# Expert loop of an attention and mixture-of-experts layer: more row and result slots, one bank for row transposes, result summed in 256 columns

## The reference

```python
x = x + attention(layernorm(x), wq, wk, wv, wo)      # 16 heads of 128, rotary, causal
h = layernorm(x)                                      # 2048 rows of 256
scores = softmax(h @ gate_w.T)                        # 8 experts
topk_w, topk_idx = top_k(scores, 2); topk_w /= topk_w.sum(-1)
y_all[e] = (silu(h @ w1[e]) * (h @ w3[e])) @ w2[e]    # 176 inner columns
y = sum over the two chosen experts of topk_w * y_all
x = x + y + (silu(h @ sw1) * (h @ sw3)) @ sw2         # shared part, 352 inner columns
```

## Time and profile before

| | us |
|---|---|
| median of 3 runs | 754.27 |
| all runs | 753.98, 754.27, 758.5 |
| span of the profiled execution | 754.1 |
| TensorE busy in it | 721.8 (96%) |
| VectorE busy | 641.8 (85%) |
| ScalarE busy | 535.6 (71%) |
| GpSimd busy | 513.2 (68%) |

### The profile page before, as it was taken

How to read it: one execution, slowest core, us unless ns; L and a number is a source line. 1 busy time by engine, 2 the same in 40 slices (tenths; PEclk the granted TensorE clock), 3 DMA queues, 4 the chain that set the end, 5 groups by cost and what they waited for, 6 DMA issues and landing times.

```text
span 754.1 us, 16244 instructions
## 1 busy us (share of the span) xinstructions
PE 721.8 (96%) x5403; PEld 682.9 (91%) x5403; DVE 641.8 (85%) x1826; ACT 535.6 (71%) x1683; POOL 513.2 (68%) x536
## 2 busy tenths in 40 slices
PE   5899999999999999999999999999999798899998
PEld 4787999999999999999999999999999787689898
DVE  6898889988998989898989988999889757688667
ACT  5788777777777777778777777777777735466474
POOL 5778567777778777877787777777766515544363
PEclk9999999999999999999999999999999999999999
DMA  6545203331322133213312330213444533334371
GB/s 205 147 159 147 100 22 112 117 112 36 118 105 101 37 128 118 80 59 133 131 45 75 134 104 22 83 51 114 183 178 163 199 102 106 112 127 125 124 277 64
DMA packets 49483, 85.90 MB, mean 114 GB/s; under 512 B 8440, under 2 KB 40152, under 8 KB 47800
## 3 DMA queue, kind: packets, MB, share of 16 engines
q1 hardware_dynamic: 45352, 73.44, 29.1%
q0 software_dynamic: 4048, 11.42, 4.2%
HBM read 60.12 MB, written 44.59 MB: 139 GB/s over the span
## 4 chain that ended last, share of the span: by engine, by line
PE 80%; DVE 9%; ACT 4%; POOL 3%; issue 2%; DMA 1%; SPq 0%; another core or an unknown queue 0%; POOLq 0%; DVEq 0%; ACTq 0%
PE bank L642 62%; PE bank L682 5%; PE bank L675 3%; PE bank L691 3%; DVE work L1018 2%; POOL work L473 1%; PE bank L896 1%; PE bank L867 1%; PE bank L898 1%; DVE work L1011 1%; PE bank L886 1%; ACT work L1433 1%; PE bank L790 1%; DVE w_lo L985 1%; PE bank L835 1%
## 5 line engine op out<-in xcount | busy, mean ns | idle before, releaser
L1639 POOL TENSOR_TENSOR qkt_lo<-work,qkt_hi 128x512 fp32r<-128x512 f32 x128 | 166.2, 1298 | 84.1 <-ACT qkt_hi L1426 84.0
L473 POOL TENSOR_TENSOR work<-work 128x512 f32<-128x512 f32 x127 | 165.4, 1303 | 47.1 <-DVE work L1018 44.1
L1018 DVE TENSOR_TENSOR work<-bank,sinn 64x512 f32<-64x512 f32 x256 | 176.2, 688 | 3.4
L642 PE MATMUL bank<-xnt_hi,w_lo 128*128 128x256 f32 x512 | 146.4, 286 | 2.3 <-DVE xnt_lo L1049 2.3
L1426 ACT CAST qkt_hi<-work 128x512 fp32r<-128x512 f32 x128 | 79.6, 622 | 96.3 <-POOL work L473 94.6
L642 PE MATMUL bank<-xnt_lo,w_hi 128*128 128x256 f32 x512 | 145.9, 285 | 0.0
L642 PE MATMUL bank<-xnt_hi,w_hi 128*128 128x256 f32 x512 | 145.8, 285 | 0.0
L1433 ACT ACTIVATE work<-work,bias 128x128 f32<-128x128 f32 (+1 forms) x256 | 112.6, 441 | 0.0
L1011 DVE TENSOR_TENSOR work<-bank,cosn 128x512 f32<-128x512 f32 x128 | 87.9, 687 | 18.6 <-PE bank L642 18.2
L642 PEld LDWEIGHTS bank<-xnt_hi,w_lo 128*128 128x128 f32 x512 | 98.8, 193 | 3.1 <-DVE xnt_lo L1049 3.1
L642 PEld LDWEIGHTS bank<-xnt_lo,w_hi 128*128 128x128 f32 x512 | 99.2, 194 | 0.0
(11 more groups left out here) (182 smaller groups left out, 2140.0 us busy)
## 6 DMA issues: line engine op xcount, KB each, us to landing
rows_by_expert<-in_zero_t SPq DMA_DIRECT2D x17, 1028.0 KB
weights_split<-stage SPq DMA_DIRECT2D x40, 176.0 KB
w_lo<-weights_split SPq DMA_DIRECT2D x4, 1408.0 KB
stage<-rows_by_expert SPq DMA_DIRECT2D x39, 128.5 KB
w_lo<-results_by_token SPq DMA_DIRECT2D x16, 256.0 KB, 4.8
w_hi<-weights_split SPq DMA_DIRECT2D x2, 1536.0 KB
stage<-in_L_ffn_w SPq DMA_DIRECT2D x32, 88.0 KB
weights_split<-stage SPq DMA_DIRECT2D x20, 128.0 KB
```

The lines of the kernel that those rows point to most:

```text
L473: eng.tensor_tensor(roped[:, a], rope_cos[:, a], rope_sin[:, a], ALU.add).then_inc(rope_add, 1)
L642: mm = pe.matmul(out, lhs[a], rhs[b], start=start and n == 0, stop=stop and n == 2, skip_group_check=more)
L1018: op = nc.vector.tensor_tensor(rope_sin[lo:lo + 64, a], p_qk[a][hi:hi + 64, :, :], sn, ALU.mult)
L1639: nc.gpsimd.tensor_tensor(qkt[a][1][:, :, :], roped[:, a], qkt[a][0][:, :, :], ALU.subtract).then_inc(qkt_lo, 1)
```

## The change

- Twelve places for rows (`ESLOTS`). The first four lie in `stage` as before; the other eight lie in the low half of the attention's output weights, so the fifth fetch waits for the last `output` (`y_ps`). Only four tiles are fetched ahead of the second plan's constants and of the rows of the next four shared tiles; the others follow these.
- Eight places for results (`YSLOTS`); the added four lie in `stage`.
- `turn_x` uses one bank (6), and waits for `low_x` of the tile before. All of the last router moves to bank 7, its steps move to iterations 1, 2 and 7, and the waits at L857 to L864 go; `turn_rows(8, 1)` and `ranks` have their own.
- `down_e` is five matmuls of 256 columns into one sum: hi by w2 high, hi by w2 low, lo by w2 high, the stack of 112 rows by w2 high, and the 48 high rows by w2 low. VectorE's addition goes; ScalarE's copy takes columns 0 to 255 and is the whole `result`.
- `plan_tiles` is cut into seven parts, for the second plan in iterations 9 to 15. The first plan runs the same instructions in the same three places.
- The rows of t = 3 are split in iteration 35, those of t = 4 in iteration 37.
- GpSimd's order: `results_out` 0; `later_first`, `sooner_first`; 1, 2; `choose`; 3, 4; `weigh`; 5; `address`; the four `send`; then 6 to 38.

```diff
-TURN, GATE, RANK = 2, 3, 9
+TURN, GATE, RANK = 1, 2, 7
-ESLOTS = 8
+ESLOTS, NEAR = 12, 4
+YSLOTS = 8
...
-        p_turn = [cut(3, P), cut(6, P)]
+        p_turn = [cut(3, P), cut(7, P)]
...
-        p_xe = [cut(6, P), cut(7, P)]
+        p_xe = cut(6, P)
...
             def tile_in(j):
+                if j == NEAR:
+                    sp.wait_ge(y_ps, B * N)
                 if j >= ESLOTS:
-                    sp.wait_ge(y_out[j % XSLOTS], 16 * ((j - ESLOTS) // XSLOTS + 1))
+                    sp.wait_ge(y_out[(j - ESLOTS) % YSLOTS], 16 * ((j - ESLOTS) // YSLOTS + 1))
...
-            for j in range(ESLOTS):
+            for j in range(NEAR):
                 tile_in(j)
             sp.wait_ge(max_done[1], B * N)
             sp.dma_start(plan_at[1][:, 0:DCONST], plan_t).then_inc(plan_in, 16)
             for t in range(S1, S1 + XSLOTS):
                 rows_in(t)
-            for j in range(ESLOTS, NF):
+            for j in range(NEAR, NF):
                 tile_in(j)
...
             def turn_x(j):
-                if j == 1:
-                    pe.wait_ge(resid_done, B)
-
-                if j == TURN + 2:
-                    pe.wait_ge(xt2_cp, B)
-                if j == GATE + 2:
-                    pe.wait_ge(logit_done, B)
-                if j == RANK + 2:
-                    pe.wait_ge(place_done, 2 * B)
+                if j >= 1:
+                    pe.wait_ge(xe_lo, j)
                 pe.wait_ge(x_got[j % ESLOTS], 16 * (j // ESLOTS + 1))
...
-                pe.matmul(p_yy[a][:, :], act_e[0][:, a, 0, :], downs_e[:, bass.ds(e, 1), 0, :], start=True, stop=False)
-                pe.matmul(p_yy[a][:, 0:D], act_e[1][:, a, 0, :], downs_e[:, bass.ds(e, 1), 0, 0:D], start=False, stop=False)
-                pe.matmul(p_yy[a][:, :], act_e[0][0:64 + E_TAIL, a, 1, :], downs_e[0:64 + E_TAIL, bass.ds(e, 1), 1, :],
-                          start=False, stop=True).then_inc(ye_ps, 1)
+                y = p_yy[a][:, 0:D]
+                hi, lo = act_e[0][:, a, 0, :], act_e[1][:, a, 0, :]
+                pe.matmul(y, hi, downs_e[:, bass.ds(e, 1), 0, 0:D], start=True, stop=False)
+                pe.matmul(y, hi, downs_e[:, bass.ds(e, 1), 0, D:2 * D], start=False, stop=False)
+                pe.matmul(y, lo, downs_e[:, bass.ds(e, 1), 0, 0:D], start=False, stop=False)
+                both, tail = act_e[0][0:64 + E_TAIL, a, 1, :], act_e[0][0:E_TAIL, a, 1, :]
+                pe.matmul(y, both, downs_e[0:64 + E_TAIL, bass.ds(e, 1), 1, 0:D], start=False, stop=False)
+                pe.matmul(y, tail, downs_e[0:E_TAIL, bass.ds(e, 1), 1, D:2 * D], start=False, stop=True).then_inc(ye_ps, 1)
...
-            def result(j):
-
-                dve.wait_ge(half_done, j + 1)
-                nc.vector.tensor_tensor(y_slot[j % XSLOTS], y_slot[j % XSLOTS], p_yy[j % 2][:, 0:D], ALU.add).then_inc(ye_cp, 1)
...
-                if j == NJ - 1:
-                    rows_low(S1)
+                if j in (NJ - 4, NJ - 2):
+                    rows_low(S1 + (j - NJ + 4) // 2)
...
-                if j in range(RANK + 1, RANK + 5):
-                    plan_tiles(1, j - RANK - 1)
+                if j in range(RANK + 2, RANK + 9):
+                    plan_tiles(1, j - RANK - 2)
...
-            def half(j):
+            def result(j):
 
                 act.wait_ge(ye_ps, j + 1)
-                if j >= XSLOTS:
-                    act.wait_ge(y_out[j % XSLOTS], 16 * (j // XSLOTS))
-                nc.scalar.copy(y_slot[j % XSLOTS], p_yy[j % 2][:, D:2 * D]).then_inc(half_done, 1)
+                if j >= YSLOTS:
+                    act.wait_ge(y_out[j % YSLOTS], 16 * (j // YSLOTS))
+                nc.scalar.copy(y_slot[j % YSLOTS], p_yy[j % 2][:, 0:D]).then_inc(ye_cp, 1)
...
             for n in range(TOP * ST):
                 send((xn2, twin)[n // ST][:, n % ST, :], n // ST, n % ST)
-                results_out(RANK + n)
-            for j in range(RANK + TOP * ST, NJ):
+            for j in range(6, NJ):
                 results_out(j)
```

More of the change, by code:

```diff
@@ L165, in build @@
         stage_all = stage[:, :, :].rearrange("p a b -> p (a b)")
-        assert ESLOTS * RW + DC * P <= NSTAGE * CH
+        results_at = NEAR * RW
+        rows_at = results_at + (YSLOTS - 4) * D
+        assert rows_at + DC * P <= NSTAGE * CH
         xs_slot = [t.rearrange("p (c s) -> p c s", c=DC)
-                   for t in (stage_all[:, ESLOTS * RW:ESLOTS * RW + DC * P], cosn[:, :], sinn[:, :], work[:, 0:DC * P])]
+                   for t in (stage_all[:, rows_at:rows_at + DC * P], cosn[:, :], sinn[:, :], work[:, 0:DC * P])]
         xs_t = [t[:, :].rearrange("p (a c s) -> p a c s", a=2, c=DC) for t in xnt_all]
@@ L173, in build @@
         acts_e = work[:, 2048:2048 + 4 * P].rearrange("p (a m) -> p a m", a=2)
-        x_slot = [stage_all[:, n * RW:(n + 1) * RW] for n in range(ESLOTS)]
-        y_slot = [v_late[n // 2][:, n % 2 * D:(n % 2 + 1) * D] for n in range(XSLOTS)]
+        far = G * GE
+        assert (ESLOTS - NEAR) * RW <= N * D
+        x_slot = [stage_all[:, n * RW:(n + 1) * RW] for n in range(NEAR)]
+        x_slot += [whl[1][:, far + n * RW:far + (n + 1) * RW].bitcast(F32) for n in range(ESLOTS - NEAR)]
+        y_slot = [v_late[n // 2][:, n % 2 * D:(n % 2 + 1) * D] for n in range(4)]
+        y_slot += [stage_all[:, results_at + n * D:results_at + (n + 1) * D] for n in range(YSLOTS - 4)]
         scaled = [stage_all[:, n * TOP * D:(n + 1) * TOP * D] for n in range(XSLOTS)]
+        assert XSLOTS * TOP * D <= rows_at
         twin = work[:, DC * P:DC * P + ST * RW].rearrange("p (t d) -> p t d", t=ST)
@@ L325, in build @@
         ye_cp = sem("ye_cp")
-        y_out = [sem(f"y_out{a}") for a in range(XSLOTS)]
+        y_out = [sem(f"y_out{a}") for a in range(YSLOTS)]
         came = [sem(f"came{a}") for a in range(NT)]
@@ L617, in result_in @@
                 sp.dma_start(back[t], src).then_inc(came[t], 16)
-            for n in range(XSLOTS):
-                sp.wait_ge(y_out[n], 16 * len(range(n, NJ, XSLOTS)))
+            for n in range(YSLOTS):
+                sp.wait_ge(y_out[n], 16 * len(range(n, NJ, YSLOTS)))
             for t in range(NT):
@@ L1105, in sequence @@
                             plan_tiles(0, 0)
+                            plan_tiles(0, 1)
                         if h == 12:
                             rows_low(1)
-                            plan_tiles(0, 1)
-                        if h == 13:
                             plan_tiles(0, 2)
                             plan_tiles(0, 3)
+                        if h == 13:
+                            for part in range(4, 7):
+                                plan_tiles(0, part)
                             mult_s(0)
@@ L1267, in plan_tiles @@
                                                  steps[:, None, :].to_broadcast([P, E, 16]), ALU.is_gt))
+                if part == 1:
                     step(nc.vector.tensor_reduce(tiles, over, AX.X, ALU.add))
@@ L1273, in plan_tiles @@
                         step(nc.vector.tensor_tensor(rest, tiles, taken[:, 0:E], ALU.subtract))
-                if part == 1:
+                if part == 2:
                     step(nc.vector.tensor_tensor(sums, (rest if late else tiles)[:, None, :].to_broadcast([P, E, E]), upto,
@@ L1286, in plan_tiles @@
                                                  ALU.mult))
-                if part == 3:
+                if part == 5:
                     step(nc.vector.tensor_reduce(tile_d, held, AX.X, ALU.add))
@@ L1290, in plan_tiles @@
                         step(nc.vector.tensor_scalar(tile_d, tile_d, taken[:, 0:1], 1.0, ALU.subtract, ALU.mult))
+                if part == 6:
                     nc.vector.tensor_scalar(result[:, 0, :], tile_x, float(E - 1), 1.0, ALU.min, ALU.mult).then_inc(done, 1)
@@ L1525, in high_x @@
                 act.wait_ge(xe_ps, j + 1)
-                nc.scalar.copy(xe_t[0][:, j % 2], p_xe[j % 2][:, 0:DC, :]).then_inc(xe_hi, 1)
+                nc.scalar.copy(xe_t[0][:, j % 2], p_xe[:, 0:DC, :]).then_inc(xe_hi, 1)
             def silu_e(j):
@@ L1591, in _ @@
                     high_x(j + 1)
-                if j == NJ - 1:
-                    rows_high(S1)
+                if j in (NJ - 4, NJ - 2):
+                    rows_high(S1 + (j - NJ + 4) // 2)
                 silu_e(j)
@@ L1599, in _ @@
                 if j >= 2:
-                    half(j - 2)
+                    result(j - 2)
                 if j == GATE:
@@ L1611, in _ @@
             silu_s(S1)
-            half(NJ - 2)
-            half(NJ - 1)
-            rows_high(S1 + 1)
+            result(NJ - 2)
+            result(NJ - 1)
             for t in range(S1 + 1, NT):
@@ L1792, in _ @@
             results_out(0)
-            results_out(1)
             later_first(B)
             sooner_first(B)
+            results_out(1)
             results_out(2)
+            choose(B)
             results_out(3)
             results_out(4)
-            choose(B)
-            for j in range(5, RANK - 1):
```

(3 more changed lines are left out.)

17 lines of the change are left out of this document (7 added, 10 removed).

## The result

The changed kernel took 764.99 us as the median of 4 runs (763.72 to 765.74), beside 756.22 us for the kernel before in the same comparison (4 runs, 753.98 to 758.5); the ratio of the runs is 1.0109, with a 95% interval of 1.0081 to 1.0138. In two later measurements it took 758.61 us (8 runs, beside 752.52 for the kernel before, ratio 1.0065, interval 1.0037 to 1.0092) and 756.83 us (one run, beside 753.89). So the change cost 1.1% in the first comparison and 0.65% in the second, where 745.5 us were forecast and the range ended at 755.

The account below looks back on a forecast made before the run. TensorE was taken as the bound, with 10.3 us of the loop stretch not its work. 754.1 - 10.3 - 1.4 + 0.8 + 0.2 + 1.6 = 745.0, rounded up by 0.5 to 745.5 us; 8-in-10 range 743 to 755 us.

Parts of the forecast that it names:

- `down_e`, 3 to 5 matmuls: Expert loop: five matmuls cost +0.02 us a tile, +0.8 us over 39; the 48-row matmul costs nothing extra.
- the rival: Fifth matmul of `down_e`: a restart at each 48-row matmul, 0.20 us a tile, 753.3 us; with 0.32, 758; chance 0.25.
- The bound: Price of the 48-row matmul from above: 2 x 0.10 us, 0.20 a tile; by the record's length 2 x 0.16, 0.32.
- the sum: Whole kernel: 754.1 - 10.3 - 1.4 + 0.8 + 0.2 + 1.6 = 745.0 us, counted from the profiled execution.
- All of the loop's non-work goes: Expert loop, iterations 2 to 36: the 10.3 us of the 81.2 us stretch that are not TensorE's work go.
- ScalarE's stops: Two "issue" waits, late ScalarE starts: 1.6 us kept in the sum; rival that they remain or move, 749.5 us, chance 0.12.
- Addition of VectorE: Expert loop: 16.4 us of VectorE work go, worth 2.5 us of TensorE's waits with their restarts.
- Router, order of GpSimd: Loop: TensorE's waits for `places` and scores go, `ranks` doesn't wait for `choose`; gain 2 us.
- Late rows: End of the kernel: rows of t = 3 and 4 split in iterations 35 and 37; gain 1.4 us.
- Ring of the single bank: Bank of `turn_x`: strict order of `low_x` and transposes lengthens tiles; at 0.3 us a tile 757 us; chance 0.08.
- Twelve places for rows: Row fetches in the loop: tile 8 is there from the start, two DMA waits go, 0.5 us.

Follow-up runs that it names:

- the ladder: The changed kernel with 48, 64, 65 and 112 rows in the fifth matmul of `down_e` by tile number modulo 4; 752.3 us (one run).
- `down_e` alone: The kernel before with only `down_e` in five matmuls of 256 columns, the last with 112 rows, and VectorE's addition gone; 751.48 us, ratio 0.9966.
- The version with 112 rows: The changed kernel with the fifth matmul of `down_e` as a stack of 112 rows instead of 48, same result; 746.15 us, ratio 0.9894.
- the last version: 112 rows in the changed kernel's fifth `down_e` matmul, eight places for rows, GpSimd's four scatters alternating with results 6 to 9; 747.93 us, ratio 0.9926.

## Why the prediction was wrong

**The step that failed** is one sentence of "`down_e`, 3 to 5 matmuls": "I take nothing, by the 112-row matmul". The row looked near, 112 against 48 rows and the same line of code, but the ladder shows that 112, 96 and 65 rows are one kind and 64, 48 and 32 another. The term is 39 x 0.33 = 12.9 us instead of 0, which puts 745.5 at 758.4 us. That the first measurement lies 6.6 us above that is not this step; one profile shows a stop of 6.0 us there.

One premise of the rival was wrong as well. That "nothing under 112 rows has run here" is not so: the shared tiles of the kernel before have matmuls of 96 rows, 0.12 us apart like their neighbours (714.46 to 714.58). They lie on the same side of the step as 112 rows and would have misled in the same way.

The Trainium skill, "TensorEngine Tiling (Array Packing)", Key Properties, had a part of the rule: changing the tiling mode drains TensorE. If a matmul of 64 rows or fewer counts as such a mode, the rows agree (0.33 us for a pair of switches in this stream, no second pair between two short matmuls side by side); which mode the chip takes, no run shows. By the same page of the Trainium skill, Available Configurations, 128x64 and 128x32 are modes of their own too. Matmuls of 64 and 32 columns cost 0.12 us like their neighbours, so either they didn't enter such a mode or the switch was free; the runs can't tell.

**The bound was right in size, its use was not.** I had both ends, 0.20 and 0.32 us a tile, the higher one from the record's length past its step; 0.33 was measured. That they meet is partly luck: the bound was 0.16 us twice, and the price is 0.09 at the entry, 0.19 at the exit and 0.05 behind. Its case was written down as 758 us, and the later measurements, 758.61 us and a single run of 756.83, are that case. But I gave it a chance of 0.25 and then cut the range at its nearer price, 755. With a rule for it and only an analogy against it this rival should, in my judgement, have had at least half, and the range its far end. The point from which it decides, 0.22 us a tile, was right as well: 0.11 us above it, times 39, is 4.3 us, and by its ratio the second measurement is 4.9 us slower than before.

**The rest of the sum held.** Without the short matmul the kernel takes 743.8 us in the profile and 746.15 in the median, where the sum gave 745.0 and the forecast 745.5. In part that is luck. The sum was one of spans and the forecast was read as a median, which is 2.0 us more; and the late starts of ScalarE, of which I kept 1.6 us, didn't come.

- *All of the loop's non-work goes*: expected stretch 71.2 us and 1.6 for ScalarE's stops. Measured 71.27 with 112 rows; the 1.6 didn't appear.
- *Addition of VectorE*: expected 2.5 less the 0.8 of the added matmuls, 1.7; `down_e` alone gave 2.6 us in the runs (0.0034 x 754, between 1.1 and 4.1), which contains the 1.7.
- *Router, order of GpSimd*: no wait of TensorE for `places`, scores or `choose` in any profile of the changed kernel. Right.
- *Late rows*: 1.4 expected, 1.5 in the trace.
- *Ring of the single bank*: refuted by the gapless 2.00 us.

**What was under-priced without harm.** Twelve places for rows were put at 0.5 us, the two waits of the earlier trace rows. In the two profiles of the kernel before these waits are 0.5 and 3.9 us, and with the four scatters together eight places cost 7.1 us, with the scatters apart 2.3. I had seen that results wait behind the scatters, but followed that only to the result slots (0.8 us), not on through landing, SyncE and fetch to the tile eight further on.

**ScalarE's stops.** I took them for the kernel's own and kept half. In the first profile of the changed kernel one of them cost 6.0 us with its clock; in the second profiles of both kernels, and in the third of the changed one, there is none. The first median lies 6.4 us above the second, but 3.7 us of that the kernel before shows too; that the stop makes the rest was only seen in one profile. What makes the stops wasn't settled.

The version with 112 rows beats both kernels: 746.15 us, 1.1% below the kernel before (interval 0.6 to 1.5%).

## What to carry to other kernels

Before a matmul is trimmed to the rows that it needs, see whether it crosses 64 rows: between full ones it pays 0.33 us here, nearly three times its own 0.12, and zero rows that keep it at 65 or more cost nothing in this stream. If short ones can't be avoided, put them side by side. Where several long DMAs are bunched on one queue, follow the results behind them through landing and refetch to the tile that needs the place, and look at the granted clock behind a wait of some microseconds: here it took a wait of 4.1 us to a price of 7.1.

## What the runs showed of the hardware

- Between matmuls of more than 64 rows (float32r, full clock), one of 32, 48 or 64 rows costs 0.09 us on entry, 0.19 at its own exit and 0.05 to 0.11 in the instruction behind. At 65, 96 and 112 rows it costs nothing extra, nor with 64 or 32 columns of the stationary operand. A second short one right behind it adds no second entry or exit.
- At the entry and the exit the stationary operand's load begins only with its own matmul (666.90 and 667.21 us), elsewhere one matmul earlier.
- After a wait of 4.1 us of TensorE the granted clock was 0.58 over the following 6.6 us, and the wait came to 7.1 us. After waits of 2.0 and 1.9 us in the second profile of the kernel before it was 0.50 for 6.8 and 3.4 us. Waits of 1.6 us and less in its first profile, and of 0.8 and 0.6 us in the last version, left it at 1.00.
- In one profile of the changed kernel ScalarE sat idle 2.54 us ahead of `silu_e` at 647.81 us, where 0.58 is usual, though its matmul is recorded as ended at 645.02; in two others of the same kernel it did not.
